# The mean square of a gated state-space layer, computed with ones standing in four column groups

## The reference

```python
zxbcdt = x @ Win.T                      # z, x, B, C and dt of each token
...                                     # convolution, silu, scan over the tokens: y, 256 values a token
yn = y * jax.lax.rsqrt(jnp.mean(y * y, axis=-1, keepdims=True) + EPS) * norm_w
y = yn * jax.nn.silu(z)
return y @ Wout.T
...
x = _layernorm(x + _L0_attn_ref(...))
x = _layernorm(x + _L0_ffn_ref(x, ...))
```

## Time and profile before

| | us |
|---|---|
| three runs | 703.23, 707.20, 707.19; median 707.19 |
| the profiled execution | 704.99, of which the span 703.2 |
| TensorE busy (matmuls / weight loads) | 638.3 (91%) / 519.3 (74%) |
| VectorE, ScalarE, POOL busy | 539.3 (77%), 478.9 (68%), 467.3 (66%) |
| sums of squares, line 771, matmul records | 32.3 in 256 |
| the scan, from the first sums of squares to the last | 61.7 to 403.4 |

### The profile page before, as it was taken

How to read it: one execution, slowest core, us unless ns; L and a number is a source line. 1 busy time by engine, 2 the same in 40 slices (tenths; PEclk the granted TensorE clock), 3 DMA queues, 4 the chain that set the end, 5 groups by cost and what they waited for, 6 DMA issues and landing times.

```text
span 703.2 us, 19658 instructions
## 1 busy us (share of the span) xinstructions
PE 638.3 (91%) x4891; PEld 519.3 (74%) x4891; DVE 539.3 (77%) x1845; ACT 478.9 (68%) x1211; POOL 467.3 (66%) x696
## 2 busy tenths in 40 slices
PE   6978999999999999999998689999999999999900
PEld 5856666666666656666666489999999999999900
DVE  3468988889888998889889667776666666878744
ACT  3757778777878778777887367665566556677824
POOL 5012468787878878788777757777745545777754
PEclk9999999999999999999999999999999999999965
DMA  9280001101111011101110123323422223556253
GB/s 251 51 296 20 2 27 36 46 29 35 36 42 47 25 34 35 47 28 38 32 43 32 40 59 86 92 79 108 98 78 72 71 70 102 165 155 190 104 188 111
DMA packets 56668, 54.50 MB, mean 77 GB/s; under 512 B 9562, under 2 KB 45918, under 8 KB 56304
## 3 DMA queue, kind: packets, MB, share of 16 engines
q1 hardware_dynamic: 45840, 33.67, 17.4%
q0 software_dynamic: 8416, 16.93, 7.1%
q10 hardware_dynamic: 2304, 2.65, 1.1%
HBM read 31.05 MB, written 22.63 MB: 76 GB/s over the span
## 4 chain that ended last, share of the span: by engine, by line
PE 69%; issue 8%; POOL 6%; ACT 6%; DVE 5%; DMA 3%; SPq 1%; DVEq 0%; ACTq 0%; POOLq 0%
PE p L682 14%; PE pl L673 10%; PE pj L511 5%; PE p L673 5%; PE p L771 4%; PE p L746 3%; PE p L717 3%; PE p L792 3%; PE p L740 3%; PE p L757 3%; POOL moe_rows L1749 2%; PE pj L519 2%; PE pj L665 2%; PE p L647 2%; PE p L519 1%
## 5 line engine op out<-in xcount | busy, mean ns | idle before, releaser
L1749 POOL DMA_INDIRECT moe_rows<-xT x135 | 134.6, 997 | 79.6 <-DVE xT L1374 51.9
L1673 POOL DMA_INDIRECT sorted_rows<-pair,slot x128 | 128.8, 1007 | 30.6 <-issue 28.4
L1131 DVE SCALAR_TENSOR_TENSOR acc<-pj,conv_w_sb,acc 128x511 f32<-128x511 f32 (+2 forms) x192 | 141.2, 735 | 7.3 <-ACT acc L902 5.3
L682 PE MATMUL p<-w,xT 128*128 x1080 | 143.5, 276 | 3.2 <-ACT xT L1048 3.0
L1048 ACT ACTIVATE xT<-pl,b_sb 128x128 f32<-128x128 f32 x360 | 102.9, 369 | 48.0 <-PE pl L673 46.0
L682 PEld LDWEIGHTS p<-w,xT 128*128 128x128 f32 x1080 | 131.4, 192 | 4.3 <-issue 4.3
L673 PE MATMUL pl<-xT 128*128 128x128 f32 x720 | 95.1, 275 | 1.6 <-DVE xT L1362 1.6
L673 PEld LDWEIGHTS pl<-xT 128*128 128x128 f32 x720 | 87.5, 192 | 1.9 <-issue 1.9
L1370 DVE TENSOR_TENSOR xT<-p,b_sb 128x128 f32<-128x128 f32 x135 | 39.3, 291 | 64.5 <-PE p L682 60.4
L1048 ACT ACTIVATE xT<-p,b_sb 128x128 f32<-128x128 f32 x180 | 51.6, 371 | 23.8 <-PE p L673 23.6
L902 ACT ACTIVATE acc<-pj,conv_b_sb,conv_w_sb 128x512 f32<-128x512 f32 x64 | 49.7, 777 | 25.1 <-PE pj L511 24.2
(11 more groups left out here) (235 smaller groups left out, 1360.6 us busy)
## 6 DMA issues: line engine op xcount, KB each, us to landing
xT<-sorted_rows SPq DMA_DIRECT2D x135, 65.0 KB, 1.9
xres<-in_x SPq DMA_DIRECT2D x16, 256.0 KB, 3.0
w<-in_w SPq DMA_DIRECT2D x2, 2048.0 KB, 10.1
acc<-moe_rows SPq DMA_DIRECT2D x12, 256.0 KB, 3.2
xT<-moe_rows SPq DMA_DIRECT2D x12, 256.0 KB, 5.5
out<-sz ACTq DMA_DIRECT2D x10, 256.0 KB, 2.1
moe_rows<-xT POOLq DMA_INDIRECT x135, 2.5
sorted_rows<-pair,slot POOLq DMA_INDIRECT x128, 2.4
```

The source lines that it names most:

```text
L682: mm = pe.matmul(y_bank(j)[:, 0:P], hT[j % 4][:, f, :], w2[:, bass.ds(e, 1), f, :].rearrange("p e d -> p (e d)"), start=(f == 0), stop=(f ...
L1131: ins = dve.scalar_tensor_tensor(out=acc[:, k, j:TOKS], in0=pj[k % 2][:, 0:TOKS - j], scalar=conv_w[:, k, TAPS - 1 - j:TAPS - j], in1=acc[ ...
L1673: pool.indirect_dma_start(out=sorted_rows[:, :], out_offset=bass.IndirectOffsetOnAxis(slot[q.par][:, c, k:k + 1], 0), in_=(rowA, rowB)[k][ ...
L1749: pool.indirect_dma_start(out=moe_rows[:, :], out_offset=bass.IndirectOffsetOnAxis(xs[k][:, P:P + 1].bitcast(I32), 0), in_=ye[j % 8], in_o ...
```

## The change

The sums are formed the other way round. A block of 32 columns of ones stands in the array and the squares pass through it, 128 tokens at a time. Chunk c goes to the column group c, so its sums come out along a row, on each of the 32 partitions 32c to 32c + 31 of p7. The halves are the outer loop now, so that neighbouring matmuls lie in different column groups. Then the sums have to come back onto the partitions: ScalarE copies the 128x128 block into a new buffer, kept, behind its first Silu activation (in pass 15, which has none, behind the last squares); TensorE turns it into the second quarter of p7, before the last chunk's output products; VectorE reads every 32nd column of that. Two semaphores are new.

```diff
+        kept = sb("kept", [P, P])
...
+        sums_kept = sem("sums_kept")
+        turned_psum = sem("turned_psum")
...
-                    for c in range(NC):
-                        for k in range(CC):
-                            mm = pe.matmul(p7[:, c * PADN:(c + 1) * PADN], ysq[:, k, c * P:(c + 1) * P],
-                                           ones[:, 0:PADN], start=(k == 0), stop=(k == CC - 1))
+                    for k in range(CC):
+                        for c in range(NC):
+                            mm = pe.matmul(p7[Q * c:Q * (c + 1), 0:P], ones[:, 0:Q], ysq[:, k, c * P:(c + 1) * P],
+                                           start=(k == 0), stop=(k == CC - 1), skip_group_check=True)
                     mm.then_inc(ss_psum, 1)
...
                         if c + 1 == NC:
+                            pe.wait_ge(sums_kept, s.n + 1)
+                            pe.transpose(p7[:, P:2 * P], kept[:, :], ident[:, :]).then_inc(turned_psum, 1)
...
+            def keep_sums(s):
+                act.wait_ge(ss_psum, s.n + 1)
+                wait(act, turned_psum, s.n)
+                act.copy(kept[:, :], p7[:, 0:P]).then_inc(sums_kept, 1)
...
+                if scan and not project:
+                    keep_sums(s)
                 if project:
                     for k in range(XC):
                         activate(q, k)
+                        if k == 0:
+                            keep_sums(s)
...
                 if scan:
-                    dve.wait_ge(ss_psum, s.n + 1)
+                    dve.wait_ge(turned_psum, s.n + 1)
                     wait(dve, rms_ready, s.n)
-                    dve.tensor_scalar(ms[:, :], p7[:, 0:NC * PADN].rearrange("p (c e) -> p c e", e=PADN)[:, :, 0],
+                    dve.tensor_scalar(ms[:, :], p7[:, P:2 * P].rearrange("p (c e) -> p c e", e=Q)[:, :, 0],
                                       1.0 / DI, EPS, ALU.mult, ALU.add).then_inc(ms_ready, 1)
```

## The result

The changed kernel takes 708.8 us (median of 9 runs, 707.46 to 710.29), the kernel before 705.21 us in runs beside it. The ratio is 1.0045, with a 95% interval of 1.003 to 1.0061: 3.2 us slower, between 2.1 and 4.3. The forecast was 709.3 us, and a sum of +3.2.

The account below looks back on a forecast made before the run. Each pass was taken as bound by a chain through TensorE, with POOL's gated block and ScalarE as close. Scan +0.6 and pass 15 +2.6 gave +3.2 us: 709.3 us, the middle of 708.2 and 710.4; range 704.5 to 714.0.

Parts of the forecast that it names:

- rival 3: The narrow sums do not run in parallel groups, so their step stays 1.90 us: 710.5 to 712 us, chance 0.07.
- Pass 15, +2.6 forecast: In the last pass the read waits behind six output products, so the expert stage begins 2.6 us later, once.
- The scan, +0.6 forecast: Over the 16 passes: ten at +0.04 and two at +0.10, the others 0, together +0.6 us.
- +0.04 a pass and +0.10 in two: Turn +0.11 us; products start 0.07 earlier in ten passes, 0.01 in passes 2 and 11.
- Pass 1, forecast at 0: POOL is early there and TensorE gains up to a microsecond, but ScalarE can give only 0.08: no change.
- ScalarE has only its 0.08 to give: ScalarE's 0.27 us wait before its second z activation shrinks to 0.08 behind the copy, the only slack left.
- a pass under 22.4 us: Sign that the forecast is wrong because POOL or ScalarE give way; the forecast pass length was 22.55 us.
- 0.08 us a record: Price taken for the narrow sums' 16 records, 1.3 us in all instead of 1.90, from a line with 64 columns.
- the favourable price: Narrow sums at 0.041 us a record, 0.66 us in all, ending at 197.9, still before POOL's block at 198.76.
- What is late next: On VectorE and POOL behind the turn: read 1.46 us later, residual 0.75, mask 0.31, next mask 0.08; cost 0.00.
- The rival that VectorE becomes the bound: The residual's 0.75 us delay passes into 12 passes: 719 us in full, 714 for half, chance 0.15.
- The rival that the narrow sums pay: If the products did not wait for POOL, 0.6 to 1.2 us saved in 14 passes: 692 to 701 us, chance 0.05.

Follow-up runs that it names:

- last_old: The changed kernel with the old form of the sums kept in pass 15 alone: 704.57 us against 705.46 before, ratio 1.0007.
- only_last: The kernel before with the sums formed in the new way in pass 15 alone: 709.38 us, ratio 1.0071 to the kernel before.
- turn_first_last: The changed kernel with the turn of pass 15 moved ahead of the output products: 704.46 us, ratio 0.9993 to the kernel before.
- gate_early: The changed kernel with POOL's fourth gated block issued ahead of the scatter before it: 703.75 us, ratio 0.9971 to the kernel before.
- sums_4x: The changed kernel with the narrow sums issued four times over, 64 records instead of 16: 711.97 us, ratio 1.0106 to the kernel before.
- both_gates: gate_early plus turn_first_last, with the two skip products moved from ScalarE to VectorE: 701.75 us, ratio 0.9941 to the kernel before.
- both_gates_z: both_gates with the inner products and second half of z swapped, and their two ScalarE steps: 702.5 us, ratio 0.9948 to the kernel before.
- early_first: The changed kernel with the edits of gate_early and turn_first_last: 701.98 us, ratio 0.9938 to the kernel before.
- before_early: The kernel before with POOL's fourth gated block ahead of the scatter: 705.63 us against 705.51, ratio 1.0.

## Why the prediction was right, and where it was off

**The direction and the place were right, the exact size was in part luck.** +3.2 us was the sum, +3.2 us the ratio, and it came from the place named: pass 15, where the read of the sums stands behind the output products and a full expert stage behind the read. `last_old` and `only_last` show this apart, and `turn_first_last` removes it. But the two terms missed in opposite directions: the scan cost nothing where 0.6 was forecast, and pass 15 cost more than 2.6 (3.7 us by the ratios of the change and `turn_first_last`, 5.0 by `only_last`). The 709.3 also stood on 706.1 for the kernel before, the mean of 704.99 and 707.19, where 705.21 was measured beside the change. The rivals' times do not all stand on that base: rival 3, worked out as the forecast is, comes to 710.0 to 711.1 and not to 710.5 to 712.

**Pass 15, +2.6 forecast.** At full clock the term is exact: in `gate_early` the read starts at 402.00, 1.81 us behind its products (weight load 400.19), and the forecast had 1.77 + 0.04. In the profile of the change it is 407.98 - 404.64 = 3.34, so 1.53 us came on top from the halved clock. With the 0.31 by which the products start later (404.64 against 404.33, the offset from before) the three make up the 4.48 of the read: 2.64 + 1.53 + 0.31. The clock was not foreseen. What failed in this term is the tacit step that the engine's speed stays what the row before showed. The ratio of the change does not show the whole 1.5, and it need not, since the kernel before loses clock in some of its runs too: of its 23 runs beside the first experiments, the seven with a mean granted clock under 0.975 took 705.9 to 708.0 us, and thirteen of the sixteen others 702.5 to 705.5. All nine runs of the change are at 0.975 or below.

**The scan, +0.6 forecast, 0.0 measured.** The two parts of an ordinary pass were right in kind. The products start right behind POOL's block (198.98, block ended 198.94), and the turn takes 0.11 us in the chain. Their net, +0.04 a pass and +0.10 in two, was mis-sized: relative to the z half ahead of them the products start 0.11 us earlier (198.98 - 196.31 against 198.87 - 196.09), not 0.07. A sum of differences of 0.04 us is below what these rows carry. Passes 2 and 11, forecast at +0.10 each, came in at +0.16 and +0.11. Pass 1, forecast at 0, gained 0.21 and evened them out. There the step "ScalarE has only its 0.08 to give" failed: it had 0.2, which its row does not show as idle. The text had named a pass under 22.4 us as a sign of being wrong, and pass 1, at 22.32, is one.

**The narrow sums.** I took 0.08 us a record and 0.041 as the most favourable, both in busy time of the matmul records. By that measure line 774 has 10.3 us / 256 = 0.040, so the favourable price came true and the 0.08 taken was twice too high. It did no harm, for the reason given: the products wait for 198.80 whatever the price. The Trainium skill (TensorEngine Tiling (Array Packing), Theoretical Speedup) has up to four times for such widths; by the weight loads it is 1.86 / 0.38, nearly five, by the matmul rows 2.02 / 0.64, three. The same page's drain on a change of mode (Key Properties) fits idle times on both sides of the narrow sums. In pass 0 their first load starts at 62.14, 0.39 us behind the squares and only as the z matmuls of line 522 end, where the wide load started at 61.48, 0.04 behind the squares. And where POOL does not hold the products, their first load stands 0.20 us behind the last narrow one, in pass 1 (85.23), in `gate_early` and in `sums_4x`, where the wide loads before followed each other without a gap. In an ordinary pass of the change the products wait for POOL anyway, and it cost nothing.

**What is late next.** With the offset of 0.22 taken off, the read, the root, the residual, the mask and the next mask are at 200.57, 200.82, 201.97, 203.05 and 205.58; forecast 200.61, 200.86, 202.0, 203.13 and 205.66. The rival that VectorE becomes the bound had its mechanism (the residual did come 0.7 late) and not its price: the idle times in front of the masks took it all.

**The rival that the narrow sums pay** was given 0.05 and is right under a condition that it named: not in this kernel, but with POOL's block early. It was worth 0.2 us a pass, not 0.6 to 1.2, because ScalarE's fourth activation is the next to hold TensorE.

## What to carry to other kernels

Where three engines finish a stage within 0.2 us of each other, making one of them faster by a microsecond changes next to nothing, and its price is paid where the stage has no cover: look at the last pass, whose queues hold other work behind the same wait. Move a read behind work only if that work's own release is early; in the last pass the turn belonged in the idle time ahead of the products. A row without an idle bracket is not a row without slack: compare the distance between two starts with the same distance in a round where the neighbour was early. Then ask what holds the stage now: here one swap on POOL turned the useless saving into a gain that the old kernel could not get from the same swap.

## What was not expected of the hardware

Sixteen loads of 32 columns in four alternating column groups took 0.38 us, 0.024 each, where 128 columns took 0.116 and 64 columns 0.052 (26.8 us / 512). And TensorE's granted clock at the end of the scan is not settled by the program: behind 1.5 us of idling in pass 15 it fell to 0.50 in the profiles of the change, of `only_last`, `turn_first_last`, `sums_4x`, `both_gates`, `both_gates_z` and `early_first`, and stayed at 1.00 in those of the kernel before, of `last_old`, `gate_early` and `before_early`, which idle there as long. The kernel before and `only_last` have the same instructions up to that point. What decides between the two is open. It was not tried to keep TensorE busy in just these gaps.
